# A fused attention and mixture-of-experts block on one core: expert banks in pairs, score blocks ahead of the last chunk, chunks between the last tile's steps

## The reference

```
x = x + attn_a(layernorm(x))   # rms norm, Q K V, elu, per-token head mixing, two rms norms, 2-layer gelu MLP
x = x + ffn(layernorm(x))      # 32 experts of width 64, softmax router, top 8, all experts computed
x = x + attn_b(layernorm(x))   # 16 heads of 8, softmax over a causal window of 64 keys, output projection
x = x + ffn(layernorm(x))      # the same experts again
```

## Time and profile before

| what | value |
| --- | --- |
| median of 3 runs | 1065.91 us (1059.64, 1065.91, 1067.04) |
| the profiled execution's own time | 1073.04 us |
| its span, first to last instruction | 1071.3 us |
| mean granted TensorE clock in it | 0.944 |
| PE, DVE, ACT, POOL busy | 950.1, 662.9, 620.5, 623.7 us |

### The profile page before, as it was taken

The page is one execution under the profiler, slowest core; times in us unless marked ns, Lnnn a source line. Parts: engine busy times, 40 slices in busy tenths (PEclk is TensorE's granted clock), DMA queues, the critical chain, the costliest instruction groups (busy, mean ns, idle before and its releaser), DMA issues.

```text
span 1071.3 us, 16672 instructions
## 1 busy us (share of the span) xinstructions
PE 950.1 (89%) x5472; PEld 657.8 (61%) x5472; DVE 662.9 (62%) x1508; ACT 620.5 (58%) x1894; POOL 623.7 (58%) x543
## 2 busy tenths in 40 slices
PE   3245999998999899999999989999999999997998
PEld 1023666676666566587666556677666666775665
DVE  5884785576877657468738567578734433476432
ACT  3236555984664584777575654697365444776422
POOL 6753787542687668534568659644565555332554
PEclk9997999878999999969999999999899999788899
DMA  5004352114333553510235444430255553010652
GB/s 172 1 0 92 79 115 46 41 41 92 90 81 82 118 130 86 114 37 16 60 82 121 102 107 108 92 76 17 45 115 119 120 131 79 21 32 22 140 121 59
DMA packets 63224, 85.67 MB, mean 80 GB/s; under 512 B 3681, under 2 KB 29090, under 8 KB 62882
## 3 DMA queue, kind: packets, MB, share of 16 engines
q1 hardware_dynamic: 63138, 84.61, 34.6%
HBM read 79.32 MB, written 5.28 MB: 79 GB/s over the span
## 4 chain that ended last, share of the span: by engine, by line
PE 58%; ACT 16%; DVE 9%; POOL 6%; issue 5%; DVEq 0%; POOLq 0%; ACTq 0%
PE bank L1362 13%; PE bank L1337 8%; PE bank L1339 7%; PE bank L1338 7%; ACT probs L928 5%; PE bank L1398 5%; PE bank L1383 5%; POOL work L762 3%; PE bank L1412 3%; DVE work L1140 2%; ACT z L808 2%; PE bank L1376 2%; DVE probsT L1181 1%; ACT work L908 1%; ACT L908 1%
## 5 line engine op out<-in xcount | busy, mean ns | idle before, releaser
L762 POOL TENSOR_TENSOR work<-work,spread_w 128x512 f32<-128x512 f32 x256 | 343.7, 1351 | 240.6 <-DVE work L1140 224.0
L1140 DVE TENSOR_TENSOR work<-work,bank 128x512 f32<-128x512 f32 x256 | 174.7, 683 | 236.8 <-ACT work L908 121.1
L1362 PE MATMUL bank<-work,down_w 128*128 128x512 f32 x512 | 262.8, 597 | 5.2 <-ACT yT L920 5.1
L908 ACT ACTIVATE work<-bank 128x512 f32<-128x512 f32 x256 | 151.7, 596 | 199.3 <-PE bank L1339 194.9
L928 ACT ACTIVATE probs<-bank,neg_max 128x96 f32<-128x96 f32 x512 | 166.7, 369 | 20.6 <-DVE neg_max L1167 16.8
L1337 PE MATMUL bank<-z_hi,gate_hi 128*128 128x512 f32 x256 | 172.1, 672 | 0.0
L770 POOL TENSOR_TENSOR probs<-probs,prob_inv 128x768 f32<-128x768 f32 x64 | 94.0, 1468 | 126.2 <-DVE prob_inv L1175 126.2
L928 ACT ACTIVATION_READ_ACCUMULATOR probs<-bank,neg_max 128x1 f32 x512 | 120.5, 236 | 0.0
L1362 PEld LDWEIGHTS bank<-work,down_w 128*128 128x128 f32 x512 | 95.6, 189 | 31.7 <-issue 11.0
L1339 PE MATMUL bank<-z_hi,gate_lo 128*128 128x512 f32 x256 | 103.2, 403 | 0.0
L1338 PE MATMUL bank<-z_lo,gate_hi 128*128 128x512 f32 x256 | 102.6, 401 | 0.0
(11 more groups left out here) (143 smaller groups left out, 1485.3 us busy)
## 6 DMA issues: line engine op xcount, KB each, us to landing
spread_w<-comb_dram SPq DMA_DIRECT2D x128, 512.0 KB, 6.7
vals<-v_dram SPq DMA_DIRECT2D x16, 384.0 KB, 3.9
x_buf<-x SPq DMA_DIRECT2D x8, 256.0 KB, 3.2
v_dram<-v_tok SPq DMA_DIRECT2D x8, 256.0 KB, 5.6
out<-xs SPq DMA_DIRECT2D x8, 256.0 KB, 3.8
spread_w<-wg SPq DMA_DIRECT2D x1, 1024.0 KB, 6.4
spread_w<-wu SPq DMA_DIRECT2D x1, 1024.0 KB, 8.5
comb_dram<-combT SPq DMA_DIRECT2D x16, 64.0 KB, 1.6
```

Source lines behind the costliest of these rows:

```text
L762: pool.tensor_tensor(work[:, n % WORK], work[:, n % WORK], spread_w[:, n // EACH % 2, s % EACH], ALU.mult).then_inc(hid_gated, 1)
L908: act.activation(work[:, n % WORK], bank[GATE_BANKS[pos % DEEP]], ACT.Silu).then_inc(silu_ready, 1)
L1140: dve.tensor_tensor(work[:, n % WORK], work[:, n % WORK], bank[UP_BANKS[position(row, f, s) % DEEP]], ALU.mult).then_inc(gated_ready, 1)
L1362: pe.matmul(bank[Y_BANK], down_w[:, c], work[:, n % WORK], start=(c == 0), stop=(c == CH - 1)).then_inc(down_done, 1)
```

## The change

1. GATE_BANKS and UP_BANKS become (0, 2, 4) and (1, 3, 5): a chunk's two banks are neighbours. A list RINGS replaces "position modulo 3". It runs 0, 1, 2 but leaves out a 0 at one place of a 32-chunk stream (position 12) and at two places of a 64-chunk stream (positions 18 and 38), so that the last three chunks of every stream use the pairs 0/1, 2/3 and 4/5. At those places two chunks in a row reuse a pair that was used two chunks before, instead of three.
2. The first score pair and its maxima are issued ahead of the last chunk of a stream. The three downs that are left over are each issued one or two score pairs later.
3. At the end of an attention: chunk 0 of the next stream goes ahead of mix of tile 6 and chunk 1 behind it; silu and gated of chunk 0 go ahead of the copies of the last tile's probsT; there is a third slot (26) between the last transposes and mix of tile 7, and proj 0 is there (in rows 0 to 2). proj 1 goes to slot 3 of "first" (slot 2 in the last period).
4. Nearly all side steps change their slot, most by two or three slots later, with some pairs set further apart (qkv, attnT behind h_sum). In the first stream mlp1 goes behind chunk 3 and mlp2 behind chunk 4; expo, elu and qscale go behind attnT. y_back of group 3 goes from slot 2 to slot 8 of attention.
5. SP issues the first half's values (`first_values`) in "fourth" for all periods but the first.

The diff at its core (of the tables the steps that the prediction names):

```diff
-GATE_BANKS, UP_BANKS = (0, 1, 4), (2, 3, 5)
+GATE_BANKS, UP_BANKS = (0, 2, 4), (1, 3, 5)
 PLAN = {
     "first": {
-        0: back(("proj", 0), ("m_stats", 2)) + own(("h_sq1", 1)),
-        1: back(("m_rstd", 2), ("proj", 1)) + own(("h_red1", 1)),
+        0: back(("m_stats", 2), ("m_rstd", 2)) + own(("h_sq1", 1)),
+        1: own(("h_red1", 1)),
+        3: back(("proj", 1)) + own(("h_newton2", 1), ("h_rg", 1)),
...
-        11: back(("weighT", 2)) + own(("h_sum", 1), ("x_add", 1)),
+        13: back(("weighT", 2)),
     "third": {
-        2: back(("m_apply", 3)) + ahead(("qkv", 5), ("h_newton1", 0)),
+        4: back(("m_apply", 3)) + ahead(("h_newton2", 0), ("h_rg", 0)),
-        11: back(("weighT", 3)) + ahead(("h_sum", 0), ("x_add", 0)),
-        12: ahead(("attnT", 0), ("kvsum", 4)),
+        9: back(("top", 3)) + ahead(("qkv", 4), ("h_sum", 0), ("x_add", 0)),
+        11: back(("comb", 3)) + ahead(("attnT", 0)),
     "attn": {
-        2: back(("y_back", 3)),
+        8: back(("y_back", 3)),
+        26: own(("proj", 0)),
 SPECIAL = {
     (0, "first"): {
-        0: own(("attnT", 1), ("mlp1", 1)) + ahead(("attend", 0)),
-        2: own(("mlp2", 1)) + ahead(("kvsum", 0)),
+        0: own(("attnT", 1)),
+        1: ahead(("expo", 0)),
+        2: ahead(("elu", 0), ("qscale", 0), ("attend", 0)),
+        3: own(("mlp1", 1)) + ahead(("kvsum", 0)),
+        4: own(("mlp2", 1), ("m_stats", 1), ("m_rstd", 1)) + ahead(("wterm", 0), ("attend", 1)),
     (ROWS, "second"): {
-        0: back(("proj", 1), ("m_stats", 3), ("m_rstd", 3)),
+        2: back(("proj", 1), ("m_stats", 3), ("m_rstd", 3)),
-        11: back(("weighT", 3)),
+        13: back(("weighT", 3)),
+RINGS = {32: [0, 1, 2] * 4 + [1, 2] + [0, 1, 2] * 6, 64: ([0, 1, 2] * 6 + [1, 2]) * 2 + [0, 1, 2] * 8}
...
@@ block.scalar and block.vector, end of an attention @@
+                    silu(*STREAM[stream_end(row)], 0)
                     turned_block(row, TILES - 1)
+                    gated(*STREAM[stream_end(row)], 0)
+                    turned(row, TILES - 1, (0,))
...
@@ block.tensor, gate_up @@
-                    if pos >= DEEP:
-                        pe.wait_ge(freed, n - DEEP + 1)
+                    if there is not None:
+                        pe.wait_ge(freed, there + 1)
                     elif after is not None and banks[ring_of_chunk] < HG:
-                        pe.wait_ge(probs_ready, tile(after, TILES) * HG)
+                        pe.wait_ge(probs_ready, tile(after, TILES - 1) * HG + banks[ring_of_chunk] + 1)
@@ block.tensor, score @@
-                    pe.wait_ge(silu_ready, stream_end(row) * CH)
-                    if pair[0]:
-                        pe.wait_ge(gated_ready, stream_end(row) * CH)
+                    free = stream_end(row) * CH - 2 + pair[0] // 2
+                    pe.wait_ge(silu_ready, free)
+                    pe.wait_ge(gated_ready, free)
@@ block.tensor, stream and attention @@
+                        if s == CH - 1 and STAGE_AT[row, f] in ENDS:
+                            score(ENDS[STAGE_AT[row, f]], 0, (0, 1))
...
+                    gate_up(*following, 0)
                     mix(row, TILES - 2)
-                    gate_up(*following, 0)
+                    gate_up(*following, 1)
                     run_steps(steps, period, place, HOOKS * TILES)
-                    gate_up(*following, 1)
```

330 lines of the change are left out of this document (171 added, 159 removed).

## The result

| kernel | median us (lowest to highest, runs) | profiled execution: span, mean granted clock |
| --- | --- | --- |
| before | 1073.45 (1059.64 to 1093.24, 20) | 1071.3, 0.944 |
| changed | 1057.72 (1047.73 to 1063.94, 20) | 1055.6, 0.955 |

The ratio is 0.9884, 95% interval 0.9851 to 0.9918: 12.4 us faster by the ratio, 15.7 us by the medians; the ratio leaves out slow executions, those over 1.5% above the fastest of the same kernel, and the medians do not. I had forecast 23 us, from a median of 1065.91 that rested on three executions; over twenty it is 1073.45. The direction holds, and 1057.72 lies in the range of 1031 to 1059, but it is 15 us above the forecast of 1043, and the size does not hold.

A forecast was written before the change was run, and what follows sets the result against it. Streams were taken as bound by PE's work, attentions costing up to 7.6 us more at low clock. Terms 14 + 0 + 4.5 + 5.6 = 24.1 us; 23 off the 1065.9 median gave 1043 us, range 1031 to 1059.

The forecast's parts named there:

- exits: Four seams out of attentions: work fills PE's waits and half clock shrinks; 14 us gained, bounds 8 and 17.
- entries: Four seams into attentions: earlier scores and maxima remove waits, others arise; sum 0, bounds -1 and +1 each.
- start: First stream: chunk 5 comes earlier as work fills PE's wait ahead of mlp1; 4.5 us gained, bounds 2 and 6.5.
- slots in the streams: Inside streams 1 and 2: PE's waits for attn_sum and yT mostly go; 4 us gained in each.
- eight ring skips: Eight places in the streams where a bank pair is reused after two chunks: 0.3 us lost each, 2.4 in all.
- I take the same for attentions 0 and 3: Seams behind attentions 0 and 3: the 4.6 us estimated behind attention 2 was assumed there too.
- Later slots for the rest of the steps cost nothing where the result is wanted a stage later: Side steps inside the streams: moving the remaining ones to later slots was priced at nothing.
- low bound of 8: Seams out of attentions: gain if all half-clock stretches stay, taken as 4 x 2.0 us.
- The wait of 0.65: Out of attention 1: PE's wait ahead of mix, counted among 3.7 us of waits and slow clock in 17.2 us.
- Rival B: Attentions: denser seams keep the clock up in one more attention, worth 7.6 us, giving 1035 us; chance 0.09.
- Rival A: Streams behind the seams: PE waits there instead; start and half the seams remain, 9 us gained, 1057; chance 0.19.

The follow-up runs named there:

- e5: Changed kernel with the end of an attention as before (chunks 0 and 1, silu, gated, proj 0 and 1 at old places): 1062.8 us, ratio to before 0.9946.
- e3: Changed kernel with the first score pair and maxima behind the last chunk again and leftover downs at old places: 1060.1 us, ratio to before 0.9869.
- e6: Changed kernel with the start and first stream in the order of before: 1061.9 us, ratio to before 0.9919.
- e9: Changed kernel with the side steps of periods 1 to 3 at their slots of before, except the two projections: 1064.9 us, ratio to before 0.9972.
- e8: e3 with bank rings by position modulo 3 again, so no pair is reused after two chunks: 1061.0 us.
- e10: Changed kernel with attention 0's y_back, norm, seq_turn and keys one slot earlier, as before: 1042.4 us, ratio to before 0.9778.
- e16_before_a0: Kernel before with the change's slots for attention 0's y_back, norm, seq_turn and keys: profiled execution 1074.22 us, the other five 1097 to 1111.
- e14_keys: Changed kernel with only seq_turn and keys of attention 0 put back to their slots of before: 1049.2 us, ratio to before 0.9784.
- e4_start: Kernel before with the change's list ahead of the first stream and its slots in stream 0, nothing else: 1061.9 us, ratio to before 0.9899.
- after_again: Second profile of the changed kernel, nothing edited: a long execution of 1085.87 us, used in no time comparison.

## Why the prediction was right or wrong

| term | forecast, us gained | measured, medians | measured at equal clock |
| --- | --- | --- | --- |
| exits | 14 | 5.3 (e5) | 6.9 |
| entries | 0 | 2.6 (e3) | -2.7 |
| start | 4.5 | 4.4 (e6) | 3.6 |
| slots in the streams | 8 | 7.4 (e9) | 10.3 |
| eight ring skips | -2.4 | 0.9 (e8) | -1.3 |
| attention 0's slots | not priced | -15.1 (e10) | -4.0 |
| all | 23 | 15.7 | 9.9 |

The measured terms do not add up: 5.5 us by the medians, 12.8 at equal clock. Each is right for one edit to one kernel, and the clock answers to all of them together.

- **The step that failed** is one the sum doesn't contain. I wrote of exits "I take the same for attentions 0 and 3", and of steps "Later slots for the rest of the steps cost nothing where the result is wanted a stage later". In attention 0 the results of y_back, the norm, seq_turn and keys are wanted within the same attention, by queries and values at slots 8 and 10 and by the scores of its second half. I had the table in the diff and looked at attentions 1 and 2 only. "Cost nothing" is the step that was wrong: these steps, moved by one slot, cost 15 us by the medians and 11 by the ratios, 11.4 of the 13.7 us in attention 0 as half clock. That the clock stays down because the results are wanted so soon is not shown; that these slots bring the half clock is, in both kernels (e10_a0_slots, e16_before_a0). Without them the change gives 24 us (e10_a0_slots). That this is my sum is luck: 10 of the 24 are clock, and the exits term is 7 to 9 us off.
- **Exits: the mechanism right, the size wrong.** This is the term of the sum that was mis-sized, 14 us against 5.3 to 6.9. Of the 14 I had counted 9 as half clock that would go. The stretches behind attentions 0 to 2 did go, and only with the new exits, but the kernel is at half clock for about 95 us with them and for 100 without (e5_exit_old), as there is more of it inside the attentions. The clock-free part, 1.2 a seam or 4.8, is about what came, by other parts than I had: 3.0 to 3.6 us of waits at three seams, none at the fourth, and 2.3 given back in the streams. Two slips stand in the working. The wait of 0.65 lies ahead of 503.50, not in the 17.2 us, and the half clock in them cost 1.3 us (514.32 to 517.16 instead of 2.2, 517.16 to 520.71 instead of 2.9), not 1.7. And the low bound of 8, "if all of them stay", should have been 4.8.
- **Streams: the size right, at other places.** Forecast were 4 us in each of two streams. In stream 1 6.3 us of waits went, attn_sum and z among them, and yT did not (2.6 us in three waits, by ACT's copy); stream 2 kept 13.2 of 14.0.
- **Start: the size right, the path not.** 4.5 against 3.6 to 4.4 in the time. But chunk 5, 4.8 us earlier, does not carry to the last chunk of stream 0, which comes at 183.7 us instead of 183.2 with the score pair of 1.1 ahead of it; what makes the 4 us is open.
- **Entries:** the sign was inside my bounds. Tile 1's masks wait for tile 0's exponentials, 0.69 us in attentions 1 to 3, 1.30 and 0.96 in attention 0, and tile 2's for tile 1's, 0.67 to 1.93. The first was in the text at 1.0, the second was not.
- **Rival B, the clock decides**, I gave 0.09. It moved the result in both directions: 10.9 us more half clock in attention 0 and 22 less in attentions 1 to 3 than in the first profile of before; of the 15.7 between the medians 9.9 are left at equal clock. My argument against it, that attention 1 fell to half clock with PE busy, was a reason to fear it instead.
- **Idle stretches and the clock.** The falls begin behind waits of 1.30 and 0.96 us at 190 to 192 us, but e14_keys waits longer in attention 0 than the changed kernel and has less half clock. The Trainium skill (TensorE: Matmul & The Clock Gate, HAM oscillation) lays throttling to idle stretches of PE. The trace agrees with where the first fall begins, not with how long the clock stays down.
- **Rival A** (gain taken back behind the seams) had 1057, the time that came. That is luck. The exits at 5.3 to 6.9 and the start at 4.4 are near its 7 and 4.5, but of the exits only 2.3 us are given back behind them; its time comes out only because two things that it left out, the slots in the streams (7.4 to 10.3 gained) and attention 0, pull against each other. What it says of an earlier start, that PE then waits further on, is seen in e4_start.

Open: what keeps the clock at half in an attention; where the start's gain in time comes from; why e4_start gains nothing at equal clock; and which of the change's parts spared attentions 1 and 3 their half clock.

## What to carry to other kernels

Price every table that the diff touches, not the one that looks like the idea: here the special table of one attention outweighed the entries, the start and the ring skips together. Where the clock falls in a stage, a shift of one slot can be worth more than the waits it removes (here 11.4 us against 2.3), so keep each part of a change as a switch of its own and time them apart. And split each run by its mean granted clock before comparing kernels that differ by 1%: at equal clock four to twelve runs gave intervals of 1.4 to 2.1 us here, though the correction itself is only as good as its slope.

## What the runs showed of the hardware

- One kernel's time follows its mean granted clock closely: 7.2 us for 0.01, from 1047.73 us at 0.968 to 1063.94 at 0.946.
- In attention 0 the places of half clock came back in a second execution (at half for 30.7, off it for 10.2 and at half for 23.9 us both times in the changed kernel), and in the kernel before with the same slots. In attention 3 they did not, and the stretch in attention 1 of the kernel before has 20.5 us in one execution and 41.0 in another.
- Half clock just ahead of a stream's first down came with the order of PE's work there: 3.4 to 6.8 us behind attentions 0, 1 and 2 in five traces with the old exits, none in fifteen with the new.
- PE at half clock goes on being busy: 28.96 of 32 us in the changed kernel, at a mean granted clock of 0.52:

```profile
202.00:234.00 32.00, 28.96 (x209) 21.84 (x205) 14.84 (x41) 19.25 (x90) 14.66 (x12) 0.52 0.00 1
```

- In one execution (after_again) the rows of stream 0 show neither level but 0.85, with PE busy for 71.8 of 74 us:

```profile
110.00:184.00 74.00, 71.76 (x242) 43.52 (x241) 53.12 (x100) 41.10 (x77) 58.02 (x46) 0.85 0.38 79
```
